# Routing weights of the experts brought to their rows by loads from DRAM, and totals in both PSUM banks

## The reference

```python
gates = jax.nn.softmax(xt @ Wg.T, axis=-1)             # 16 experts
scores, inds = jax.lax.top_k(gates, TOP_K)             # 2 of them
scores = scores / jnp.sum(scores, axis=-1, keepdims=True)
g = jnp.einsum('td,ehd->teh', xt, We_gate)             # 64 hidden rows per expert
u = jnp.einsum('td,ehd->teh', xt, We_up)
h = jax.nn.silu(g) * u
y_all = jnp.einsum('teh,edh->ted', h, We_down)
y_sel = jnp.take_along_axis(y_all, inds[:, :, None], axis=1)
y = jnp.sum(y_sel * scores[:, :, None], axis=1)
shared = jax.nn.silu(xt @ Ws_gate.T) * (xt @ Ws_up.T) @ Ws_down.T    # 256 hidden rows
y = y + jax.nn.sigmoid(xt @ Wsg.T) * shared
```

## Time and profile before

| | us |
|---|---|
| time before, median of 3 runs (lowest to highest) | 1810.72 (1809.93 to 1811.16) |
| the profiled execution, its own time | 1810.67 |
| its span, from the first to the last instruction | 1809.4 |
| stage d, from the first gate product to the end of the span | 1554.8 to 1809.4 |
| PE busy of the whole span | 1568.5 |
| DVE, ACT, POOL busy | 1285.6, 1101.3, 698.2 |

### The profile page before, as it was taken

How to read it: one execution, slowest core, us unless ns; L and a number is a source line. 1 busy time by engine, 2 the same in 40 slices (tenths; PEclk the granted TensorE clock), 3 DMA queues, 4 the chain that set the end, 5 groups by cost and what they waited for, 6 DMA issues and landing times. The chain is left out here.

```text
span 1809.4 us, 45598 instructions
## 1 busy us (share of the span) xinstructions
PE 1568.5 (87%) x19728; PEld 1003.6 (55%) x19728; DVE 1285.6 (71%) x2035; ACT 1101.3 (61%) x1642; POOL 698.2 (39%) x500
## 2 busy tenths in 40 slices
PE   4577998999999999999977778878888888899999
PEld 2354666778777778777853323433433332566665
DVE  4665745876787687777768768778778886766564
ACT  3265667777777777786733577677677678433321
POOL 4112301544354255425531555556465555301100
PEclk8798998999999999999996989999999999999999
DMA  7864200000000000000142462164236222000000
GB/s 180 198 181 109 41 5 12 2 2 2 1 2 2 2 2 2 2 2 2 48 110 62 146 155 72 48 187 95 71 116 143 72 71 72 1 7 12 7 12 12
DMA packets 43357, 102.59 MB, mean 57 GB/s; under 512 B 3944, under 2 KB 12288, under 8 KB 41428
## 3 DMA queue, kind: packets, MB, share of 16 engines
q1 hardware_dynamic: 40244, 94.17, 20.2%
q10 hardware_dynamic: 2912, 5.51, 1.8%
HBM read 67.42 MB, written 31.46 MB: 55 GB/s over the span
## 5 line engine op out<-in xcount | busy, mean ns | idle before, releaser
L1450 DVE TENSOR_REDUCE arena<-ring 128x2 f32<-128x1024 f32 (+2 forms) x320 | 342.1, 1111 | 88.8 <-PE ring L1307 63.4
L1550 ACT ACTIVATE arena<-ring 128x1024 f32<-128x1024 f32 (+1 forms) x320 | 291.6, 938 | 129.2 <-PE ring L1336 90.2
L1357 PE MATMUL accs<-arena 128*9 128x512 f32 (+3 forms) x1536 | 174.3, 528 | 2.7 <-ACT arena L1550 2.6
L2514 POOL TENSOR_TENSOR arena<-arena 128x1280 f32<-128x1280 f32 x28 | 65.3, 2332 | 287.0 <-PE accs L2275 231.7
L1329 PE MATMUL ring<-arena 51*128 51x512 bf16 (+3 forms) x768 | 124.4, 342 | 46.6 <-DVE arena L1450 24.9
L1300 PE MATMUL ring<-arena 48*128 48x512 bf16 (+3 forms) x768 | 126.6, 342 | 41.9 <-DVE arena L1450 21.7
L2506 POOL TENSOR_TENSOR arena<-arena 128x512 f32<-128x512 f32 x112 | 141.4, 1292 | 3.0 <-DVE arena L2316 3.0
L292 POOL TENSOR_SCALAR xn<-x,moments,rstd 128x128 f32<-128x128 f32 x80 | 64.4, 814 | 198.2 <-DVE rstd L263 182.6
L2781 ACT ACTIVATE arena<-ring 128x512 f32<-128x512 f32 x80 | 47.8, 598 | 147.2 <-PE ring L2636 142.6
L2499 POOL TENSOR_TENSOR arena<-arena 128x1024 f32<-128x1024 f32 x32 | 86.2, 2694 | 108.2 <-DVE arena L2373 108.2
L2741 DVE TENSOR_TENSOR arena<-arena,ring 128x512 f32<-128x512 f32 x80 | 55.0, 688 | 87.8 <-PE ring L2638 74.2
(11 more groups left out here) (346 smaller groups left out, 4225.8 us busy)
## 6 DMA issues: line engine op xcount, KB each, us to landing
arena<-whole_k SPq DMA_DIRECT2D x32, 512.0 KB, 4.6
arena<-whole_q SPq DMA_DIRECT2D x32, 512.0 KB, 6.2
arena<-c_scratch_q SPq DMA_DIRECT2D x14, 384.0 KB, 10.2
arena<-c_scratch_k SPq DMA_DIRECT2D x14, 384.0 KB, 13.3
a_scratch_k<-arena SPq DMA_DIRECT2D x8, 512.0 KB
c_scratch_k<-arena SPq DMA_DIRECT2D x8, 512.0 KB, 3.8
arena<-a_scratch_q SPq DMA_DIRECT2D x9, 384.0 KB, 7.2
arena<-a_scratch_k SPq DMA_DIRECT2D x9, 384.0 KB, 9.5
```

What stands on the lines that cost most here:

```text
L1357: mm = nc.tensor.matmul(acc[ci % 2][32 * h:32 * h + HD + 1, a - c * BANK:BANK], c_values[b % 2][:, j, r * HEADS // 2 + 2 * g + i, :], weig ...
L1450: nc.vector.tensor_reduce(dst, src, AX.X, ALU.max, negate=True).then_inc(c_max_taken.up(item), 1)
L1550: nc.scalar.activation(view(c_probs[wi % 4]), view(ps), ACT.Exp).then_inc(c_weights_made.up(item), 1)
```

## The change

It takes the spreading away from PE. The 17 weights of each token stay in float32: the eight transposes give 17 rows of 1024 tokens (moe_rows), SP writes them to a DRAM tensor (moe_scratch), and SP loads them back, each expert's row into the 64 partitions of its expert (function sp_spread). A piece is the weights for one tile of one half: 128 partitions x 512 tokens in float32, 256 KB, and there are nine pieces for the ten blocks of a half, since the two shared tiles use the same one. Four buffers for pieces (moe_spread) lie in SBUF space of stage c that is no longer used. DVE's second multiplication (now L2748) takes the piece in place of the PSUM bank. The bank that the product used is free, and the totals of the halves take turns in the two banks. Splits and the matrix of zeros and ones are gone.

```diff
@@ the order
-                       ("top", b), ("first", b), ("rest", b), ("next", b), ("weigh", b), ("split", b, 0), ("split", b, 1),
-                       ("rows", b)])
+                       ("top", b), ("first", b), ("rest", b), ("next", b), ("weigh", b), ("rows", b)])
...
-            42: [("split", 0, 0)], 43: [("split", 0, 1)], 47: [("rows", 0)]}
+            43: [("rows", 0)]}
@@ PE
-                pe.wait_ge(moe_rows_made, b)
-                pe.wait_ge(constants_made, "all")
-                if i:
-                    pe.wait_ge(hidden_step, (moe_blocks[i - 1], "weighed"))
-                else:
-                    pe.wait_ge(c_copied, batches * GROUPS * HALVES - 1)
-                e = min(f, EXPERTS // 2)
-                nc.tensor.matmul(moe_spread[:, :], w3["moe_bcast"][:, e * P:(e + 1) * P], moe_T[b % 2][:, cols],
-                                 start=True, stop=True).then_inc(hidden_mm.up((item, "spread")), 1)
...
-                if f == 0 and i:
-                    pe.wait_ge(moe_added, moe_blocks[i - 1][1:3])
+                if i == 0:
+                    pe.wait_ge(c_copied, batches * GROUPS * HALVES - 1)
+                if f == 0 and i >= 2 * MOE_TILES:
+                    pe.wait_ge(moe_added, moe_blocks[i - MOE_TILES - 1][1:3])
@@ DVE
-                dv.wait_ge(hidden_mm, (item, "spread"))
+                k = piece_of(*item[1:])
+                dv.wait_ge(spread_there(k), ("spread", k))
...
-                nc.vector.tensor_tensor(hid[i % 3][:, :], a, moe_spread[:, :], ALU.mult).then_inc(
+                nc.vector.tensor_tensor(hid[i % 3][:, :], a, moe_spread[k % 4][:, :], ALU.mult).then_inc(
@@ SP, new
+        def sp_spread(k):
+            b, h, g = moe_pieces[k]
+            rows = slice(EXPERTS, NG) if g == EXPERTS // 2 else slice(2 * g, 2 * g + 2)
+            n = rows.stop - rows.start
+            if k >= 4:
+                sp.wait_ge(hidden_step, (last_user(k - 4), "weighed"))
...
+            sp.wait_ge(moe_scratch_there, b)
+            nc.sync.dma_start(moe_spread[k % 4][:, :], moe_scratch[b, rows, h * BANK:(h + 1) * BANK].unsqueeze(1).to_broadcast(
+                [n, P // n, BANK])).then_inc(spread_there(k).up(("spread", k), 16), 16)
@@ in moe_sp
+            if kind == "rows":
+                b = item[1]
+                sp.wait_ge(moe_rows_made, b)
+                nc.sync.dma_start(moe_scratch[b], moe_rows[:, :]).then_inc(moe_scratch_there.up(b, 16), 16)
+            for k in moe_fetch_at.get(item, []):
+                sp_spread(k)
```

More of the change, by code:

```diff
@@ L2553, in build @@
         xnT_d = [xnT_0, xnT_2]
[L2554 to L2556 removed]
+        stack_words = HEADS // 2 * T // 2
+        assert used[0] <= stack_words
+        used[0] = 2 * stack_words
+        moe_spread = [carve([P, BANK]) for i in range(4)]
+        moe_scratch = nc.dram_tensor("moe_scratch", (batches, NG, T), F32, kind="Internal").ap()
+        moe_cleared, moe_scratch_there = signal("moe_cleared"), signal("moe_scratch_there")
         moe_step, moe_turned, moe_rows_made = signal("moe_step"), signal("moe_turned"), signal("moe_rows_made")
@@ L2598, in build, with moe_fetches @@
         moe_at = {item: i for i, item in enumerate(moe_blocks)}
-        moe_total, moe_spread = acc
+        moe_total = lambda b, h: acc[(b * HALVES + h) % 2]
+        moe_pieces = [(b, h, g) for b in range(batches) for h in range(HALVES) for g in range(EXPERTS // 2 + 1)]
+        piece_of = lambda b, h, f: moe_pieces.index((b, h, min(f, EXPERTS // 2)))
+        last_user = lambda k: ("hidden", *moe_pieces[k][0:2], MOE_TILES - 1 if moe_pieces[k][2] == EXPERTS // 2 else moe_pieces[k][2])
+        spread_there = lambda k: stack_there[k // 2 % 2, k % 2]
+        def moe_fetches():
+            at, written, waiting = {}, set(), list(range(4))
+            for item in [("rows", 0)] + moe_order():
+                if item[0] == "rows":
+                    written.add(item[1])
+                elif item[0] == "down":
+                    waiting += [k for k in range(4, len(moe_pieces)) if last_user(k - 4) == ("hidden", *item[1:])]
+                at[item] = [k for k in waiting if moe_pieces[k][0] in written]
+                waiting = [k for k in waiting if k not in at[item]]
+            assert not waiting
+            return at
+        moe_fetch_at = moe_fetches()
         def moe_wait_free(item):
@@ L2724, in moe_dve @@
                                         ALU.mult).then_inc(step("weights"), 1)
[L2725 to L2732, removed]
             elif kind == "rows" and b == 0:
                 dv.wait_ge(moe_turned, (b, "rows"))
-                nc.vector.tensor_copy(moe_T[0][:, :], ps[:, :]).then_inc(moe_rows_made.up(b), 1)
+                nc.vector.tensor_copy(moe_rows[:, :], ps[0:NG, :]).then_inc(moe_rows_made.up(b), 1)
             elif kind == "hidden":
```

34 lines of the change are left out of this document (14 added, 20 removed).

## The result

Eight timed runs, four of each kernel: 1925.8 us after (1924.3 to 1929.0) against 1810.9 us before (1809.9 to 1813.7). The ratio is 1.063, with a 95% interval of 1.062 to 1.065: the changed kernel is 115 us slower. The profiled run took 1926.2 us, its span is 1924.8 us. The forecast was 1935 us.

A forecast was written before the change was run, and what follows sets the result against it. PE was taken to bound stage d before, two-engine loads after: 369.4 us of loads and writes from 1550.4, 10.0 us behind them, 4 for clock and 1.3 over span give 1935 us; range 1900 to 2040.

The forecast's parts named there:

- Number of engines: Stage d's expert-tile loads: each runs on 2 DMA engines, by the source's slowest level of 2, not 16.
- Speed of one engine: Expert loads in stage d: 24.4 GB/s per engine, so 5.37 us a piece, 343.7 us for 64 pieces.
- Slow reading of a repeated row: Rival for stage d's loads: two engines, up to 8.3 us a piece; chance 0.19 up to 2040, shared with low clock.
- the sum: Work of the two engines in stage d: expert pieces, shared pieces, stores of x, writes and idle time, together 369.4 us.
- Start and writes: Before and in stage d: first write issued about 1544.5, first load bytes 1550.4; three later writes 8.6 us plus 6.0 idle.
- The end: End of stage d: last expert piece in at 1919.8 us, then 10.0 us, so the span ends at 1929.8.
- The clock: PE's granted clock falls in stage d's gaps between blocks: 4 us lost, between 0 and 70.
- the gain: Stage d on PE: 80 removed spread products of 0.22 us save 17.6 us, on the path in nearly all of it.
- the rival of sixteen engines: Stage d's loads run on 16 engines, PE stays the bound: time 1794 us (1788 to 1802); chance 0.12.

The follow-up runs named there:

- the version without loads: Changed kernel with only the first four pieces of spread weights loaded and used in turn by all blocks; 1802.1 us, 0.994 of before.
- the version with sixteen engines: Changed kernel with two experts' rows interleaved in the packed weights, so a load reads its two rows in turn, 64 times; 1802.1 us, 0.9945 of before.
- the version without the product: Kernel before with the spread product of the first block only, 79 of 80 left out; 1800.9 us, 0.994 of before.

## Why the prediction was right

**Number of engines.** The step on which all hung. 260 more small packets in the changed kernel, 1156 more (5100) with the order of rows turned round, as the prediction had them for two and for sixteen engines. The three-row and four-row transfers of before were the right neighbours, not the loads with 16 or more rows. The rule of the Trainium skill (DMA: Bandwidth & Descriptors, section Why a DMA increments its semaphore by 16 and not by 1), the largest number up to 16 that divides the slowest count of both sides, fits every count of this case, if the numbers that lie side by side inside a row are not taken for a level: a write of one row of 1024 numbers, not repeated, leaves one small packet.

**Speed of one engine.** 5.37 us a piece was forecast from rows 6; 5.28 us is the usual distance between blocks, 64 x 0.09 = 5.8 us less in all. Slow reading of a repeated row (rows 7, 15.8 GB/s) does not exist here: two engines carry 50 GB/s. Distances near 5.9 stand mostly where the packets of a store of x crossed the two engines, once where a shared piece and a fetch of instructions did, and once behind a write. All of this but the fetch was in the sum.

**Start and writes.** The first write is issued at 1547.5, not 1544.5, and the first bytes of a load move at 1553.5 in place of 1550.4: 3.1 us later. The forecast way from the write to the first load (5.9 us) was right. The last score product of the attention starts at 1510.5 where before had it at 1507.4 (L1300 there), so the 3.1 us were there before the work that the prediction timed. Versions with the same program up to there have 1500.6 to 1513.5, so no edit is shown to be the cause. The three writes with their idle time were forecast at 8.6 + 6.0 = 14.6 us; the gaps are 11.3 us.

**The end.** The weighing of the last expert piece was forecast for 1920.3 (1919.8 and the landing) and starts at 1915.4. The terms account for it: +3.1 for the start, -5.8 for the pieces, -3.3 for the gaps. The +1 that is missing is a difference, not read: stores and shared pieces are left for it. The tail from there to the end of the span is 9.4 us, forecast 9.5.

**The clock.** 4 us were added for it, and this term was not needed. The clock does fall, to 0.86 or 0.91 over 40 us, and the gate product takes 698 ns at the mean in place of 595. But PE at the full clock has some 2.7 of 5.28 us to spare in each expert block, so it is early at VectorE's weighing all the same. 1.3 us for the time over the span is what the run showed (1926.2 - 1924.8 = 1.4). So 1935 - 4.9 - 4 = 1926.1.

**Where a step was mis-sized: the gain.** The prediction took 80 x 0.22 = 17.6 us for the removed products, "on the path in nearly all of stage d". With two engines this was covered by the loads and did not show. With enough engines it did: the way through the stage is 11.6 us shorter with sixteen, and the time 7 to 12 us. In the profile the start of stage d, 3.1 us later than before (1560.6 against 1557.5), takes the rest: 1810.7 - 11.6 + 3.1 = 1802.2. The 0.22 us per block is right where a block has PE alone; at the three turns PE waits for GpSimd, and at the second (in some versions at the third too) it then runs at a lower clock. So the rival of sixteen engines, had it come true, would have ended at about 1802 us, at the top of its 1788 to 1802. Rows 1 had a sign of it: 38.65 us of PE in 40 in the window with the turn, against 40.00 in the one without.

**What stays open.** Why the version without loads spreads over 1793 to 1811 us in ten runs: the records show granted clocks between 0.949 and 0.958 over the span, and the lower ones go with the longer times. Its one profile says where: against the version with sixteen engines it is early by 9.4 us already at the first product of stage c (L943, 871.7 against 881.1), and over the first 200 us its granted clock is 0.89 against 0.85. Why the same program is granted more clock in one run than in another stays open. That VectorE's weighing held GpSimd back (820 to 841 ns at the mean for a tile of L287, 789 for L292 of before, 799 for it in the version without the product) is seen in the versions with both inputs in SBUF; it was not separated from the rest.

## What to carry to other kernels

Before a product is replaced by a load, work out on how many DMA engines that load runs: look at the small packets that each DMA leaves at its end, find the slowest level of source and destination, and multiply by the rate of one engine, not of all. A broadcast of few rows is the bad case, and the cure is cheap: one DMA for each row, or an order in which the repeats are the outer level. And a saving on the engine that bounds a stage counts only for those blocks in which it waits for nobody; take the blocks beside side work out of the sum.

## What the runs showed of the hardware

- The most frequent recorded time of a packet on one engine: 27 ns for 512 B (stores of x), 46 for 1 KB (bf16 loads), 84 for 2 KB (loads), 159 for 4 KB (writes), which is about 8 ns and 19 ns for each 512 B. Two packets of 1 KB thus take 10% longer than one of 2 KB.
- One row and 17 rows behave alike: splitting each of four writes into 16 rows and 1 row took the small packets from 4204 to 4268, so a write of 16 rows leaves sixteen, and one of a single 4 KB row leaves one, as one of 17 rows does. A row read 128 times over leaves sixteen.
- SyncE itself is held when the engines of its loads are behind. These are the traces' entries for the loads' issues in the changed kernel and in the version with sixteen engines (duration in ns: min, median and max), and the timeline of the changed kernel behind the second write:

```profile
L2811 SPq DMA_DIRECT2D arena<-moe_scratch x72: 487/3896/5952, 1552.2 to 1900.6; - x72
```

```profile
L2813 SPq DMA_DIRECT2D arena<-moe_scratch x72: 465/513/809, 1553.2 to 1783.6; - x72
```

```profile
1633.72 0.26 SPq L2819 DMA_DIRECT2D moe_scratch<-arena  x1
1643.10 9.36 SPq L2811 DMA_DIRECT2D arena<-moe_scratch  x4
1652.51 5.13 SPq L2826 DMA_DIRECT2D x_out<-x  x1
```

In the changed kernel an issue lasts 487 ns at the least, 3.9 us at the median, and the four behind the write 9.36 us together. The store of x stood in the same queue behind loads: its own issue took 5.13 us, and stores landed 12.7 us after their issue (median), against 2.3 us in the version with sixteen engines. Nobody waits for these stores but the last, which comes after all loads; in a kernel that needs them sooner the two engines could cost more than their own loads, which no run here tried.
